# The first group of four heads is taken as two halves of two heads, and the order of all steps is written anew

## What is computed

```python
x = x + 0.5 * _L0_ffn_ref(_layernorm(x), L0_ffn_weight_q, ...)    # quantised to int8
x = x + _L0_attn_ref(_layernorm(x), L0_attn_W_KQV, L0_attn_W_O)   # 16 heads of 8, rotary
x = x + 0.5 * _L0_ffn_ref(_layernorm(x), ...)
x = x + 0.5 * _L1_ffn_ref(_layernorm(x), ...)                     # gated
x = x + _L1_attn_ref(_layernorm(x), ...)                          # 16 heads of 64
x = x + 0.5 * _L1_ffn_ref(_layernorm(x), ...)

# _L0_attn_ref
scores = jnp.einsum('bhqd,bhkd->bhqk', Q, K) / sqrt(d)
scores = jnp.where(causal, -jnp.inf, scores)
probs = jax.nn.softmax(scores, axis=-1)
heads = jnp.einsum('bhqk,bhkd->bhqd', probs, V)
```

## Time and profile before

| | us |
|---|---|
| median of 3 runs | 786.88 |
| lowest, highest | 783.63, 787.39 |
| profiled execution, its own time | 787.15 |
| its span | 785.4 |

### The profile page before, as it was taken

How to read it: one execution, slowest core, us unless ns; L and a number is a source line. 1 busy time by engine, 2 the same in 40 slices (tenths; PEclk the granted TensorE clock), 3 DMA queues, 4 the chain that set the end, 5 groups by cost and what they waited for, 6 DMA issues and landing times.

```text
span 785.4 us, 21560 instructions
## 1 busy us (share of the span) xinstructions
PE 718.6 (92%) x9387; PEld 428.2 (55%) x9387; DVE 532.5 (68%) x730; ACT 454.4 (58%) x535; POOL 467.1 (59%) x367
## 2 busy tenths in 40 slices
PE   3667988889888899999999999999999999999997
PEld 1433535345344454655555566645776655557764
DVE  7599888998878785778587645665645655643037
ACT  2425876987776679554746546556544565563502
POOL 6814546522841210499989759978457967689630
PEclk9955998999889999999999999999999999999999
DMA  8000000000000000001001101110110110112100
GB/s 275 2 1 2 4 1 3 3 3 3 3 1 3 2 3 2 3 3 30 22 10 29 29 2 30 30 29 3 29 30 3 29 30 3 29 29 57 29 1 28
DMA packets 13226, 16.20 MB, mean 21 GB/s; under 512 B 3053, under 2 KB 10573, under 8 KB 13133
## 3 DMA queue, kind: packets, MB, share of 16 engines
q1 hardware_dynamic: 12556, 14.50, 6.6%
q10 hardware_dynamic: 576, 0.33, 0.1%
HBM read 13.26 MB, written 1.17 MB: 18 GB/s over the span
## 4 chain that ended last, share of the span: by engine, by line
PE 74%; DVE 11%; ACT 9%; issue 3%; POOL 1%; DMA 1%; SPq 0%; ACTq 0%; DVEq 0%; POOLq 0%
PE ps L1261 20%; PE ps L1210 17%; ACT Pr L697 7%; DVE big L1074 7%; PE ps L1181 6%; PE ps L1425 5%; PE ps L1240 5%; PE ps L1464 3%; PE ps L1432 3%; PE ps L1382 2%; PE ps L1271 2%; PE ps L1376 2%; PE ps L1251 1%; PE ps L1221 1%; PE ps L1231 1%
## 5 line engine op out<-in xcount | busy, mean ns | idle before, releaser
L697 ACT ACTIVATE Pr<-ps,exp_scale 128x1024 f32<-128x1024 f32 (+1 forms) x294 | 278.8, 1006 | 122.2 <-PE ps L1261 74.1
L679 POOL TENSOR_TENSOR V0s<-V0s,Pr 128x1024 f32<-128x1024 f32 x77 | 181.4, 2356 | 106.4 <-PE ps L1210 60.6
L1105 DVE TENSOR_REDUCE mxb<-ps 128x8 f32<-128x1024 f32 (+1 forms) x152 | 173.6, 1163 | 86.0 <-PE ps L1261 66.5
L1074 DVE TENSOR_REDUCE big<-ps 128x8 f32<-128x1024 f32 (+1 forms) x159 | 170.2, 1116 | 22.7 <-PE ps L1240 16.0
L1261 PE MATMUL ps<-big 64*128 64x128 f16 (+2 forms) x2560 | 168.3, 259 | 0.9 <-DMA big<-turns 0.7
L1240 PE MATMUL ps<-big 32*128 32x128 f16 (+2 forms) x1280 | 105.1, 280 | 32.9 <-DVE big L1074 15.6
L1261 PEld LDWEIGHTS ps<-big 64*128 64x128 f16 x2560 | 92.8, 94 | 71.0 <-issue 23.9
L1210 PE MATMUL ps<-Pr,V1s 128*64 128x128 f32 (+2 forms) x960 | 110.2, 370 | 0.0
L1240 PEld LDWEIGHTS ps<-big 32*128 32x128 f16 x1280 | 42.5, 95 | 108.8 <-ACT Pr L697 44.0
L679 POOL TENSOR_TENSOR acts<-acts,Pr 128x1024 f32<-128x1024 f32 x35 | 82.4, 2355 | 22.3 <-PE ps L1210 12.4
L1210 PEld LDWEIGHTS ps<-Pr,V1s 128*64 128x64 f32 x960 | 57.0, 136 | 41.4 <-issue 28.2
(11 more groups left out here) (242 smaller groups left out, 915.7 us busy)
## 6 DMA issues: line engine op xcount, KB each, us to landing
rec_b<-scratch_dram SPq DMA_DIRECT2D x30, 256.0 KB, 3.9
X<-in_x_dram SPq DMA_DIRECT2D x2, 256.0 KB, 3.6
big<-in_pick_rows_dram SPq DMA_DIRECT2D x2, 256.0 KB, 3.5
X<-in_x_dram SPq DMA_DIRECT2D x1, 512.0 KB, 5.6
rec_b<-in_w_q_dram SPq DMA_DIRECT2D x1, 512.0 KB, 6.0
XT<-in_w_k_dram SPq DMA_DIRECT2D x1, 512.0 KB, 6.8
XT<-in_w_v_dram SPq DMA_DIRECT2D x1, 512.0 KB, 7.6
wo_s<-in_w_o_dram SPq DMA_DIRECT2D x1, 512.0 KB, 8.5
```

Of the source, the lines that this page charges most:

```text
L679: g.tensor_tensor(dst, dst, src, ALU.add).then_inc(summed, 1)
L697: ins = a.activation(dst[:, part], src, func, scale=scale)
L1074: ins = v.tensor_reduce(maxima_of(mall[:, r, 2 * u:2 * u + 2][:, part], i), block_view(src, i), AX.X, ALU.max, negate=True)
L1105: ins = v.tensor_reduce(maxima_of(mxb[:, r][:, part], arg), block_view(src, arg), AX.X, ALU.max, negate=True)
```

## The change

Group 0 alone is taken in halves: first all nine maxima tiles of heads 0 and 1, then those of heads 2 and 3. Behind each nine DVE makes the minima of two heads (three small operations on half as many values), and each half has a step `gturn` with a turning, a copy and two DMAs of its own, and two semaphores (`first_shift`) for them. Its exponentials come in the same order, nine of half 0, then nine of half 1, and it has 18 weighings of one chunk and two heads in place of nine of four heads. Groups 1 to 7 stay as they are. The counts that others wait for (`pv0`, `mx0_ready`, `shift0_set`) are shifted to match. The string `ORDER` has ten more letters and is written anew from start to end; of it the diff shows two lines.

```diff
...
     halves = [(i, u) for i in range(CH) for u in range(2)]
+    first = [(i, u) for u in range(2) for i in range(CH)]
     return {
         "a": [("gkq", g, None, "AV") for g in range(G)],
-        "m": [("gmax", g, at, "V") for g in range(G) for at in halves],
-        "t": [("gturn", g, None, "A") for g in range(G)],
-        "e": [("gexp", g, at, "A") for g in range(G) for at in halves],
-        "w": [("gweigh", g, i, "") for g in range(G) for i in range(CH)],
+        "m": [("gmax", g, at, "V") for g in range(G) for at in (halves if g else first)],
+        "t": [("gturn", 0, u, "A") for u in range(2)] + [("gturn", g, None, "A") for g in range(1, G)],
+        "e": [("gexp", g, at, "A") for g in range(G) for at in (halves if g else first)],
+        "w": [("gweigh", 0, at, "") for at in first] + [("gweigh", g, i, "") for g in range(1, G) for i in range(CH)],
         "g": [("gheads", g, None, "V") for g in range(G)],
...
 ORDER = (
-    "ammmmmmmmammmmmmmmmmamtmmehemehmhmemememmmweehmwemmwemwemewemehwmehewemhthweaemehweemwegemehwmemwemm"
-    "emwemwmehmewmmhmemhmewmeemetmmhmhmwhhmmhmememwmeegemwememhhwmmehhhewemwaemwememwhemmhetmwemememwmeme"
...
+    "ahmmmmmmmahhmmmtmmamemeehwmmwemwememmewwmemhtwhmehewmmhwmehwewemwemwmewmmewmwehmwmemmhamwtmmhmememwe"
+    "mewmeemehwmemwemhwemhhmmhhhmmwemeemmeegmwtemmemwememhemwhmwmemwememehmmwemamewemegeemwmeehwemwemwmem"
...
 )
...
 BANKS_OF, USERS_BEFORE = deal_banks()
+
+
+def group_exp_no(g, i, u):
+
+    return 2 * CH * g + 2 * i + u if g else CH * u + i
+
+
+def group_weighed(e_no):
+
+    return e_no + 1 if e_no < 2 * CH else 2 * CH + (e_no - 2 * CH) // 2 + 1
 
...
         mxs = spare[:, 576:640].bitcast(F16).rearrange("p (r w h t) -> p r w h t", r=2, w=2, h=GH)
+        mxs_first = spare[:, 576:608].bitcast(F16).rearrange("p (u w h t) -> p u w h t", u=2, w=2, h=2)
         sht0 = spare[0:2 * GH * T, 640:768].bitcast(F16).rearrange("p (r c) -> p r c", r=2)
...
         mx0_ready, shift0_set = sem("mx0_ready"), sem("shift0_set")
+        first_shift = [sem(f"first_shift_{u}") for u in range(2)]
         pv0, acc0_saved = sem("pv0"), sem("acc0_saved")
...
                         row, src = SHIFT_ROW + part, GH * T * part
-                        sp.dma_start(QT[key % SETS][row:P:HR, :], sht0[src:src + GH * T, key % 2]).then_inc(shift0_set, 16)
+                        if key == 0:
+                            src = 2 * T * part
+                            rows = slice(row + 2 * HR * arg, 2 * HR * (arg + 1), HR)
+                            sp.dma_start(QT[0][rows, :], sht0[src:src + 2 * T, arg]).then_inc(first_shift[arg], 16)
+                        else:
+                            sp.dma_start(QT[key % SETS][row:P:HR, :], sht0[src:src + GH * T, key % 2]).then_inc(shift0_set, 16)
                 if kind == "turn":
...
             def save_heads(g):
-                act.wait_ge(pv0, CH * (g + 1))
+                act.wait_ge(pv0, CH * (g + 2))
                 if g:
...
                 if kind == "gturn":
-                    copy_out(n, sht0[:, key % 2], slot[0][0:2 * GH * T, 0:P // 2].bitcast(F16))
+                    if key:
+                        copy_out(n, sht0[:, key % 2], slot[0][0:2 * GH * T, 0:P // 2].bitcast(F16))
+                    else:
+                        copy_out(n, sht0[0:4 * T, arg], slot[0][0:4 * T, 0:P // 2].bitcast(F16))
                 if kind == "gexp":
...
                         save_heads(key - 1)
-                    e_no = 2 * CH * key + 2 * arg[0] + arg[1]
+                    e_no = group_exp_no(key, *arg)
                     if e_no >= GROUP_BUFS:
-                        act.wait_ge(pv0, (e_no - GROUP_BUFS) // 2 + 1)
+                        act.wait_ge(pv0, group_weighed(e_no - GROUP_BUFS))
                     copy_whole(n, group_buf[e_no % GROUP_BUFS], ACT.Exp, exp_scale[0][:, 0:1])
...
                     if (key, arg) == (0, 0):
-                        act.wait_ge(pv0, CH * G)
+                        act.wait_ge(pv0, CH * (G + 1))
                     g_no = (CH - BASE) * key + arg - BASE
...
                     ins.then_inc(slot_dve, 1)
-                    if arg == (CH - 1, 1):
+                    if i == CH - 1 and (u == 1 or key == 0):
+                        at = slice(0, GH) if key else slice(2 * u, 2 * u + 2)
                         dve.wait_ge(slot_dve, READS["V"][n])
-                        link(v.tensor_reduce(mxn[:, r], mall[:, r], AX.X, ALU.min))
-                        link(v.tensor_scalar(mxs[:, r, 0], mxn[:, r], 1.0 / SHIFT_TOP, None, ALU.mult))
-                        v.scalar_tensor_tensor(mxs[:, r, 1], mxn[:, r], 1.0 / SHIFT_TOP, mxs[:, r, 0], ALU.mult,
+                        link(v.tensor_reduce(mxn[:, r, at], mall[:, r, at], AX.X, ALU.min))
+                        high, low = ((mxs[:, r] if key else mxs_first[:, u])[:, w] for w in range(2))
+                        link(v.tensor_scalar(high, mxn[:, r, at], 1.0 / SHIFT_TOP, None, ALU.mult))
+                        v.scalar_tensor_tensor(low, mxn[:, r, at], 1.0 / SHIFT_TOP, high, ALU.mult,
                                                ALU.subtract).then_inc(mx0_ready, 1)
...
 
-            def weigh_group(g, i):
-
-                pe.wait_ge(slot_act, read("A", "gexp", g, (i, 1)))
+            def weigh_group(g, i, u=None):
+
+                pe.wait_ge(slot_act, read("A", "gexp", g, (i, 1 if u is None else u)))
                 if i == 0 and g:
...
                     half = a0 // 512
-                    for j in range(GH):
-                        src = group_buf[(2 * CH * g + 2 * i + j // 2) % GROUP_BUFS][:, j % 2, off:off + a1 - a0]
+                    for j in range(GH) if u is None else (2 * u, 2 * u + 1):
+                        src = group_buf[group_exp_no(g, i, j // 2) % GROUP_BUFS][:, j % 2, off:off + a1 - a0]
                         ins = te.matmul(ps[HR * j:HR * j + 2 * VW, ACC0, a0 - 512 * half:a1 - 512 * half],
...
                 if kind == "gweigh":
-                    weigh_group(key, arg)
+                    weigh_group(key, *(arg if key == 0 else (arg,)))
                 if kind == "weigh":
...
                 if kind == "gturn":
-                    pe.wait_ge(mx0_ready, key + 1)
-                    ins = te.transpose(slot[0][0:2 * GH * T, 0:P // 2].bitcast(F16),
-                                       mxs[:, key % 2].rearrange("p w h t -> p (w h t)"), idh_s[:])
+                    pe.wait_ge(mx0_ready, key + 2 if key else arg + 1)
+                    if key:
+                        ins = te.transpose(slot[0][0:2 * GH * T, 0:P // 2].bitcast(F16),
+                                           mxs[:, key % 2].rearrange("p w h t -> p (w h t)"), idh_s[:])
+                    else:
+                        ins = te.transpose(slot[0][0:4 * T, 0:P // 2].bitcast(F16),
+                                           mxs_first[:, arg].rearrange("p w h t -> p (w h t)"), idh_s[:])
                 if kind == "gexp":
-                    if arg == (0, 0):
-                        pe.wait_ge(shift0_set, 32 * (key + 1))
-                        if key == 0:
-                            pe.wait_ge(acc_zeroed, 1)
+                    if key == 0 and arg[0] == 0:
+                        pe.wait_ge(first_shift[arg[1]], 32)
+                        pe.wait_ge(acc_zeroed, 1)
+                    if key and arg == (0, 0):
+                        pe.wait_ge(shift0_set, 32 * key)
                     r = key % SETS
...
```

More of the change, by code:

```diff
@@ L185 @@
 ORDER = (
[L186 to L195 removed]
+    "ahmmmmmmmahhmmmtmmamemeehwmmwemwememmewwmemhtwhmehewmmhwmehwewemwemwmewmmewmwehmwmemmhamwtmmhmememwe"
+    "mewmeemehwmemwemhwemhhmmhhhmmwemeemmeegmwtemmemwememhemwhmwmemwememehmmwemamewemegeemwmeehwemwemwmem"
+    "temamhmwemwemmemwememwhememewememegewemmemwehmwmemtwmemwemememwmeegmahmmheewhwemhewemetmemehwmeehwem"
+    "wmemwemewmemwmemhemhaehwhemwemmeewehmewmeewmehtmemwemmewmmheegemhhhhwhhewemeheewwehmehwmemwememewmem"
+    "wemeemheewgQQtKKVewMeMwMeewMegeVMeweMeweMeweMeweMewMeeTweMKQwwMMgEEEEMWWMEMWMEEMWWThMEMWMEEhhhKQWWWE"
+    "MMWSEMMWWMMEVEMhTWMWMEEEEMWhWMEMWMMQKVMWhSMEEEEEMWEMMWEMhTWMEMWWMMEVhQKTWWWhWMEEMWEMEWWMMEWWSWhMEEEE"
+    "KQMhWWWMEEWMEEMWMEETSVMVhEMWWMEEhhhWWhhhWWWMEEEMWWMMhhhKQTWWSEMEWMEMWMEMWMMVhEEWWMEEEKQWWEESMEMWWTME"
+    "EMWEMMWWWQKVWMEMWEMMWWMEEEESWTMEEMWWWMEMWMMVKQWEEEMWWEEEMWWSTMMWWMEEWWMEMWEMMWEEEEESWWWMEEMVQVQOKTOM"
+    "MMWWWMMOEMMWWMMEKOSMEEEMWWWMEEEEWTKQWWWMMEWWMEEEEVEMWMhWWWEMEVTSMWMEMhWWWMEMWEEEEEMWSEEMWMMQVKhTWWWE"
+    "MWMMQKWWMEMWEEMWWMEEEMWMEEMTSWWWWMEMWMEWMEEEEEMWWWMMMWWWSThVEEEEhhhWWWEEEEEEWSOWWWWWEEOhOhOhWWW"
 )
```

8 lines of the change are left out of this document (removed).

## The result

The changed kernel is slower: 794.06 us in the median of 4 runs (790.83 to 794.34), against 785.25 (783.05 to 787.39) for the kernel before beside it. The ratio is 1.0103, 95% interval 1.0064 to 1.0142. That is 6 to 9 us, not the 1 us of the forecast. The profiled execution took 794.34 us, its span is 792.5 us, 7.1 longer than before.

The account below looks back on a forecast made before the run. PE was taken to bound the stretch to the 42nd maximum, its added 8.8 us eating the 9.4 us earlier start. Landmark 0 plus debt 1 gave +1 us, 788 for the median; range 779 to 794.5, the forecast's own 784 to 791.

Parts of the forecast that it names:

- Half weighings, +8.8 us: Group 0: a two-head weighing lasts as long as a four-head one, 0.98 us, adding 8.8 us to PE at full clock.
- The start, first exponential at 55 to 56 us: Start of group 0: with only nine maxima needed, the first exponential comes at 55.5 us, 9.4 us sooner.
- Clock rise near 63: PE's clock rises near 63 us instead of 77.2, so the low clock adds 3.75 us to the landmark.
- late-clock rival: Clock still rises at 77.2 us because half-width weighings make PE's activity thinner: +7.1 us, 795 us; chance 0.17.
- PE's busy time to 325, up by some 4 us: PE's busy time to 325 us: 8.8 us of weighings less what the low clock no longer costs.
- The landmark, unmoved at 102.7: Start of the 42nd maximum tile on DVE: PE's extra 8.8 us eat the 9.4 us of the earlier start.
- The sum: Time to the 42nd maximum: 55.5 us, plus 43.5 of PE work with 5% idle, plus 3.75 for low clock: 102.7.
- DVE's floor: Earliest time DVE's own busy time allows for the 42nd maximum tile: 96.4 us, taken as no tighter bound than PE.
- Behind the landmark, +1 us with bounds of 0 and 5: After the 42nd maximum: owed work is mostly hidden in idle time from 104 to 245 us, costing 1 us.
- the debt: Work owed at the 42nd maximum, six exponentials and 2.5 weighings; rival that it isn't hidden: +5, 792 us, chance 0.15.
- a sign that would prove me wrong: A changed number of low-clock stretches between 104 and 245 us; fewer were priced as a gain, to 779.5, chance 0.22.
- the forecast's number: Whole kernel: +1 us on the profiled execution's 787.15, so 788 us for the median; chance 0.38 within 0.5%.

Follow-up runs that it names:

- halves_apart: Kernel before in its own order, each weighing of group 0 cut in two of two heads, one score tile between; 796.60 us, ratio 1.0126.
- before_less: Kernel before, weighings of heads 2 and 3 of group 0 left out in chunks 1 to 7 but for two-column matmuls; 787.85 us, ratio 1.0022.
- after_again: The changed kernel measured once more, unchanged; 792.09 us, ratio 1.0075 to the kernel before.
- debt_first: Changed kernel to its 42nd maximum, then the owed exponentials and weighings among four maxima, then the old order; 796.15 us, ratio 1.0105.
- pool_waits: Changed kernel with POOL waiting at four steps for DVE's small operations behind a group's last maximum; 787.31 us, ratio 1.0011 to the kernel before.
- before_no_block: Kernel before with DVE's small scaling of the finished maxima written as scalar_tensor_tensor; 787.42 us, ratio 0.9995.
- stats_first: Kernel before with DVE's first small statistics step moved ahead of the first maximum; 787.12 us, ratio 0.9998.
- no_block: Changed kernel with DVE's small scaling of the finished maxima written as scalar_tensor_tensor; 793.64 us, ratio 1.0080 to the kernel before.
- before_pool_waits: Kernel before with POOL made to wait for DVE at two places, near 115 and 205 us; 787.40 us, ratio 1.0020.
- less_weighing: Changed kernel, half weighings of heads 2 and 3 of group 0 left out for chunks 1 to 7 but for one two-column matmul each; 795.38 us, ratio 1.0117.

## Why it came out slower

**Half weighings, +8.8 us: right.** 1.04 us at full clock and 1.90 at the low one, predicted 0.98 and 1.84. halves_apart measured all nine as 9.2 us at the 42nd maximum; before_less confirmed the reason.

**The start, first exponential at 55 to 56 us: right**, 54.59. **Clock rise near 63: right**, 62.0. The late-clock rival is out. **PE's busy time to 325, up by some 4 us**: from 38.4 to 325 it is 251.07 us against 248.23, up by 2.8.

**The landmark, unmoved at 102.7: too late by 3.5 us**, at 99.2. The sum took PE as the bound with 5% of idle. The window of the changed kernel from the first to the 42nd maximum shows PE idle 15% and DVE 6%:

```profile
38.24:99.20 60.96, 51.73 (x619) 26.89 (x619) 57.45 (x79) 32.57 (x40) 32.31 (x45) 0.80 0.01 2
```

DVE's floor (96.4 in the prediction) was the nearer bound, and PE needed less than I summed: from 55.5 us on it is busy 40.3 us with the low clock's part in it, where the sum had 41.5 and 3.75 for the low clock. Against halves_apart, which pays for the same halves, the 42nd maximum comes 12.6 us sooner, not 9.4; but there the changed kernel owes its six exponentials and 2.5 weighings, and halves_apart doesn't, so this isn't the worth of the early start alone.

**Behind the landmark, +1 us with bounds of 0 and 5: this is the step that failed.** At the 84th maximum both orders have done the same exponentials and weighings. From the 42nd to there the changed kernel took 71.1 us against 60.2 (67.8 in after_again), so it stands 7.5 us behind, and from there to the end of the span both take 622 us. The whole of the span's 7.1 is lost by the 84th maximum.

The bounds counted only what PE and ACT owed, and took the idle time from 104 to 245 us to hide most of it. debt_first shows the debt at 8.1 us when it is paid at once, above the 5 that I called the most, and pool_waits, with three of the stops gone, still takes 6.5 us longer than before between the two maxima. So the debt was priced too low. And the bounds held nothing for two things. First, a new order also moves POOL's and DVE's instructions against each other, and they can hold each other up: 5.3 us of stops in place of 1.8, with gaps on PE behind the two longest. pool_waits takes three of the four away (at 64.3 us one of 1.72 stays) and gets 5.6 us of the median back (4.8 beside after_again). Stops alone don't rank the kernels: debt_first has 2.8 us of them and is no faster than the changed kernel. Second, the clock: 41 us at half speed behind 104 us (31 in after_again) in place of 17. I had named this number as a sign that would prove me wrong, but priced it as a gain alone; no rival had extra low stretches on the slow side, though a sentence said that new gaps can come.

How the 5.6 us divide can be estimated from all runs. A straight line through times and mean clocks gives at clock 0.963: 786.8 us for the kernel before (122 runs, with before_no_block, stats_first and before_less, whose times don't differ), 791.9 for the changed one (22 runs, with no_block) and 788.6 for pool_waits (12). So the waits are worth 3.3 us at equal clock, and the rest goes with the clock. The figure hangs on the line taken: with the slope of the kernel before (5.1 us for 0.01 of clock) for all and the ten runs of the changed kernel alone it is 2.0. The higher clock of pool_waits isn't luck of one execution: its twelve runs have 0.963 to 0.974, the ten of the changed kernel 0.955 to 0.965.

That the stops cause the low clock is not shown. In both traces of the changed kernel a low stretch begins within 2 us of the stop near 119 us and within 5 us of the one near 180. But near 121 us one begins without a stop too: at 121.4 in pool_waits and at 121.9 in before_pool_waits, where the small operation took 0.18 us; with a stop ahead of it, it begins at 121.6 in the kernel before and at 120.1 in the changed one. Windows from the start of each to its end, pool_waits, before_pool_waits and the changed kernel:

```profile
121.40:124.80 3.40, 3.40 (x33) 1.18 (x31) 2.19 (x5) 1.67 (x3) 3.32 (x2) 0.50 0.00 0
121.90:128.70 6.80, 6.31 (x46) 4.84 (x50) 4.63 (x6) 0.43 (x2) 6.64 (x4) 0.50 0.02 5
120.10:126.90 6.80, 4.74 (x33) 1.92 (x33) 5.59 (x8) 2.30 (x3) 3.51 (x2) 0.50 0.00 0
```

**With three stops gone the forecast's number holds.** pool_waits measures 1.0011 (0.9992 to 1.0031), +1 us where the sum said +1. That is partly luck: the landmark was 3.5 us too late in the sum, what is lost behind it too small, and the higher clock helps; at equal clock pool_waits stays 1.8 to 2.6 us above the kernel before. What stays open is how it makes up the 3.1 us that it is behind at the 84th maximum: in its profile it takes 617 us from there to the end, both the kernel before and the changed one 622. Nor is settled what PE time saved in this stretch is worth: less_weighing, with an estimated 6.9 us of weighings fewer (7 x 0.98), gained nothing in its time, at a lower clock and with the early stop; by the same lines it would be 1.3 to 2.2 us below no_block at equal clock. No version beat the kernel before.

## What to carry to other kernels

A new order changes more than who waits for whom: list where GpSimd's long instructions fall against VectorE's short ones that a chain hangs on, in the order as in the trace, and try making the long one wait where POOL has time. Time it: the waits gave 5 us in one order and nothing in the other. When a new order leaves work to be done later, don't take idle time elsewhere as room for it: the debt here was priced at 1 us and cost 8 where it was paid at once. Price a change of the clock in both directions. When work is split into calls that run side by side on strips of PE, count the columns of one strip, not the matmuls.

## What the hardware showed that I had not expected

- VectorE's operation on 16 or 32 values a lane (0.17 to 0.22 us) took 0.75 to 2.29 us in 36 places of the 14 traces, in two different forms alike. Each time a TENSOR_TENSOR of GpSimd on 1024 values a lane had started before it, and it ended 0.03 to 0.05 us behind that one. With VectorE ahead by 0.26 us at 49.6 it took its 0.21 us.
- PE busy 14.00 of 14.00 us at a granted clock of 0.51 (144 to 158 us), in a stretch where after_again shows clock 1.00: the same program, 3.3 us apart at the 84th maximum and 2.7 at the end of the span.
- With seven half weighings fewer the stretch from 77.2 to 102.7 us ran at a mean clock of 0.80 in place of 1.00, and nothing was gained (less_weighing).
